# A fused four-layer graph network: the GAT keys' logit parts by token, turned into rows by transposes, in another order of the round

## The reference, cut to what matters

```python
def _L3_gnn_ref(h, adj_matrix, W, a):
    Wh = jnp.einsum('bnf,fo->bno', h, W)
    a1, a2 = (a[:Fout, 0], a[Fout:, 0])
    s1 = Wh @ a1                       # the query's part of a logit
    s2 = Wh @ a2                       # the key's part
    e = s1[:, :, None] + s2[:, None, :]
    e = jnp.where(e >= 0, e, ALPHA * e)
    e = jnp.where(adj_matrix[None] == 0, -jnp.inf, e)
    attention = jax.nn.softmax(e, axis=-1)
    h_prime = jnp.einsum('bij,bjo->bio', attention, Wh)
    return h_prime
```

## Time and profile before

| | before |
|---|---|
| median of 3 runs | 2158.94 us |
| the profiled execution: its time, and its span from first to last instruction | 2162.29 us, 2160.5 us |
| PE busy | 2017.1 us, 93% |
| DVE busy | 1749.8 us, 81% |
| ACT busy | 1451.9 us, 67% |
| mean granted TensorE clock | 0.98 |

### The profile page before, as it was taken

One profiled execution on the slowest core, in us unless ns is written; L12 is line 12 of the kernel. 1 busy time (PEld: TensorE's weight loads), 2 busy tenths in 40 slices (PEclk: granted clock), 3 DMA queues, 4 the chain that ended last, 5 costly groups with the idle time before them and its releaser, 6 DMA issues. The chain is left out here.

```text
span 2160.5 us, 86772 instructions
## 1 busy us (share of the span) xinstructions
PE 2017.1 (93%) x37609; PEld 1780.4 (82%) x37609; DVE 1749.8 (81%) x4987; ACT 1451.9 (67%) x4411; POOL 187.0 (9%) x259
## 2 busy tenths in 40 slices
PE   6979769999999999999999999999999999999986
PEld 3434358989898989889898989898989998899985
DVE  6779767888888888888888888888888888888865
ACT  5657336767776777667676776676767766676775
POOL 2000000000001000100010000101010001000000
PEclk9989789999999999999999999999999999999998
DMA  7847300000100001000100010000000010000000
GB/s 277 289 173 267 107 11 12 13 12 3 41 3 22 3 3 42 12 12 3 42 13 12 3 41 13 12 3 28 16 22 3 3 42 12 12 3 12 3 12 12
DMA packets 36825, 87.85 MB, mean 41 GB/s; under 512 B 2416, under 2 KB 26992, under 8 KB 32752
## 3 DMA queue, kind: packets, MB, share of 16 engines
q1 hardware_dynamic: 36464, 82.56, 11.0%
HBM read 52.15 MB, written 30.41 MB: 38 GB/s over the span
## 5 line engine op out<-in xcount | busy, mean ns | idle before, releaser
L1443 ACT ACTIVATE pool_mem<-ps,lstm_b 128x64 f32<-128x64 f32 (+2 forms) x2496 | 603.9, 354 | 191.8 <-PE ps L252 186.4
L250 PE MATMUL ps<-hl_a,w_hi 128*128 128x64 f16 (+2 forms) x3776 | 545.6, 215 | 31.9 <-DVE hl_a L623 16.0
L251 PE MATMUL ps<-hl_a,w_hi 128*128 128x64 f16 (+2 forms) x3776 | 544.3, 215 | 0.0
L252 PE MATMUL ps<-hl_a,w_lo 128*128 128x64 f16 (+2 forms) x3776 | 543.8, 215 | 0.0
L250 PEld LDWEIGHTS ps<-hl_a,w_hi 128*128 128x128 f16 x3776 | 350.5, 98 | 64.0 <-DVE hl_a L623 17.1
L251 PEld LDWEIGHTS ps<-hl_a,w_hi 128*128 128x128 f16 x3776 | 350.2, 98 | 24.4 <-issue 3.0
L252 PEld LDWEIGHTS ps<-hl_a,w_lo 128*128 128x128 f16 x3776 | 350.2, 98 | 24.4 <-issue 3.0
L250 PE MATMUL ps<-hl_b,w_hi 128*128 128x84 f16 (+2 forms) x2112 | 366.3, 228 | 2.5 <-ACT pool_mem L1443 1.7
L251 PE MATMUL ps<-hl_b,w_hi 128*128 128x84 f16 (+2 forms) x2112 | 366.0, 228 | 0.0
L252 PE MATMUL ps<-hl_b,w_lo 128*128 128x84 f16 (+2 forms) x2112 | 364.3, 228 | 0.0
L250 PE MATMUL ps<-pool_mem,w_hi 128*128 128x64 f16 (+2 forms) x3072 | 352.4, 200 | 2.2 <-DVE pool_mem L1716 2.0
(11 more groups left out here) (244 smaller groups left out, 4402.1 us busy)
## 6 DMA issues: line engine op xcount, KB each, us to landing
xa<-in_x SPq DMA_DIRECT2D x32, 512.0 KB, 5.5
h_scratch<-pool_mem SPq DMA_DIRECT2D x14, 1024.0 KB, 4.3
pool_mem<-h_scratch SPq DMA_DIRECT2D x14, 1024.0 KB, 6.8
pool_mem<-in_wpack SPq DMA_DIRECT2D x16, 704.0 KB, 4.3
out<-xb SPq DMA_DIRECT2D x16, 512.0 KB, 3.4
o_scratch<-act_in SPq DMA_DIRECT2D x14, 512.0 KB, 3.2
act_in<-o_scratch SPq DMA_DIRECT2D x14, 512.0 KB, 5.4
row<-in_rows SPq DMA_DIRECT2D x1, 1408.0 KB, 11.4
```

The source lines that it names most:

```text
L250: nc.tensor.matmul(o, l[0], r[0], start=first, stop=False, skip_group_check=True)
L251: nc.tensor.matmul(o, l[0], r[1], start=False, stop=False, skip_group_check=True)
L252: return nc.tensor.matmul(o, l[1], r[0], start=False, stop=last, skip_group_check=True)
L1443: op = nc.scalar.activation(gates[s][h][:, g, m * w:(m + 1) * w], gate_place(s, h, g, m, w), ACT.Tanh, bias=lstm_b[:, bias:bias + 1], scal ...
```

## The change

The keys' parts are no longer made as rows. `wa` holds the two columns side by side, and the 12 small matmuls of `gat` have two moving columns, so that s1 and s2 of a token lie next to each other on the token's partition. DVE scales all four numbers of a half (two blocks of 128 tokens by two parts) in one instruction. A new step `gat_keys` has PE turn s2 into rows: a transpose of the one column, broadcast to 128, into the same PSUM bank. ACT adds s1 as before, without a scale. ACT takes Wh out in step `gat`, ahead of the logits, which now belong to `gat_keys`; so do the leaky ReLU and the mask on DVE. The setup makes `wa` in place of `wa1` and `wa2`.

```diff
-                    for k in range(KT):
-                        product(ps[s][:, BANK_B[h], 0:HTOK], (wa2[:, 0, k, :], wa2[:, 1, k, :]),
-                                (src[:, 0, k, tokens(h)], src[:, 1, k, tokens(h)]), k == 0, k == KT - 1)
                     for b in range(HALF):
                         a = h * HTOK + b * P
                         for k in range(KT):
-                            mm = product(ps[s][:, BANK_B[h], HTOK + b:HTOK + b + 1],
+                            mm = product(ps[s][:, BANK_B[h], HTOK + 2 * b:HTOK + 2 * b + 2],
                                          (src[:, 0, k, a:a + P], src[:, 1, k, a:a + P]),
-                                         (wa1[:, 0, k:k + 1], wa1[:, 1, k:k + 1]), k == 0, k == KT - 1)
+                                         (wa[:, 0, k, :], wa[:, 1, k, :]), k == 0, k == KT - 1)
                     mm.then_inc(gat_ps.of(s, h), 1)
                     dense(s, h, src, h * HTOK, "w3", BANK_A[h]).then_inc(gat_ps.of(s, h), 1)
+
+                def gat_keys(s, n, h):
+                    pe.wait_ge(*logit_ok.at(s, n, h, "parts"))
+                    for b in range(HALF):
+                        mm = nc.tensor.transpose(ps[s][:, BANK_B[h], b * P:(b + 1) * P],
+                                                 part_of(s, h, b, 1).broadcast_to([P, P]), ident[:, :])
+                    mm.then_inc(gat_ps.of(s, h), 1)
...
                 def gat_logits(s, n, h):
 
-                    act.wait_ge(*logit_ok.at(s, n, h, "s1"))
+                    act.wait_ge(*gat_ps.at(s, n, h, "keys"))
                     for b in range(HALF):
                         op = nc.scalar.activation(logit[s][h][:, b, :], ps[s][:, BANK_B[h], b * P:(b + 1) * P], ACT.Identity,
-                                                  bias=s1[s][h][:, b:b + 1], scale=-UNSCALE)
+                                                  bias=part_of(s, h, b, 0))
...
                     elif base == "gat":
+                        take_wh(s, n, h)
+                    elif base == "gat_keys":
                         gat_logits(s, n, h)
-                        take_wh(s, n, h)
...
+                def gat_parts(s, n, h):
+                    at = 8 + (s * HALVES + h) * HALF * 2
+                    dve.wait_ge(*gat_ps.at(s, n, h, "parts"))
+                    nc.vector.tensor_scalar(small[:, at:at + 2 * HALF], ps[s][:, BANK_B[h], HTOK:HTOK + 2 * HALF], -UNSCALE, None,
+                                            ALU.mult).then_inc(logit_ok.of(s, h), 1)
...
-0:turn_state.0 1:mix1.0 1:inp1.1 1:cell1.1 0:gat.1 0:norm_l2.0 1:hid1.1 0:gat_exps.1 1:gcn1.0 0:turn_att.1 0:turn_xc.0
...
+1:mix0.0 1:inp0.1 0:turn_xc.1 0:turn_state.0 1:cell0.1 1:gcn0.0 0:gat.1 0:gat_keys.1 1:mix1.0 1:hid0.1 0:gat_exps.1
+1:inp1.1 1:cell1.1 0:norm_l2.0 1:hid1.1 0:turn_att.1 1:gcn1.0 0:turn_xc.0 0:gat_mix.1 0+norm_y 1:inp0.0 1:cell0.0
```

More of the change, by code:

```diff
@@ L89 @@
[L89 to L103, removed]
+1:cheb.1 0:pack3.1 0:cell3.0 1:conv.1 0:hid3.0 1:v.0 1:q.0 1:k.0 1:norm_g1.1 0:inp4.1 0:pack3.0 1:xa_bias.1
@@ new lines @@
+1:turn_x1.1 0:cell4.1 1:scores.0 0:inp4.0 0:cell4.0 0:hid4.1 1:v.1 1:q.1 1:k.1 0:hid4.0 0:inp5.0 1:scores.1 1:exps.0
+1:exps.1 0:inp5.1 0:cell5.1 0:cell5.0 0:hid5.1 1:turn_probs.1 0:inp6.1 1:attend.1 0:hid5.0 0:cell6.1 0:hid6.1
+1:attn_out.1 1:norm_g2.1 1:turn_probs.0 0:inp6.0 0:pack4.1 1:attend.0 0:cell6.0 1:turn_x2.1 0:inp7.1 0:cell7.1
+0:hid6.0 1:attn_out.0 0:hid7.1 0:inp8.1 0:pack4.0 1:norm_g2.0 1:mlp_up.1 1:gelu_split.1 0:cell8.1 0:inp7.0 0:hid8.1
+1:turn_x2.0 0:cell7.0 1:mlp_down.1 0:hid7.0 0:inp9.1 0:cell9.1 1:norm_g3.1 1:norm_l1.1 1:mlp_up.0 1:gelu_split.0
@@ new lines @@
+0:hid9.1 0:inp10.1 0:inp8.0 0:cell8.0 1:mix0.1 0:hid8.0 1:mlp_down.0 0:cell10.1 1:norm_g3.0 0:hid10.1 1:gcn0.1
+0:inp9.0 1:mix1.1 1:norm_l1.0 0:cell9.0 0:hid9.0 0:turn_state.1 1:gcn1.1 0:inp10.0 0:cell10.0 0:hid10.0 0:norm_l2.1
+1:mix0.0 1:inp0.1 0:turn_xc.1 0:turn_state.0 1:cell0.1 1:gcn0.0 0:gat.1 0:gat_keys.1 1:mix1.0 1:hid0.1 0:gat_exps.1
+1:inp1.1 1:cell1.1 0:norm_l2.0 1:hid1.1 0:turn_att.1 1:gcn1.0 0:turn_xc.0 0:gat_mix.1 0+norm_y 1:inp0.0 1:cell0.0
+0:norm_l3.1 0:gat.0 0+turn_y.1 0:gat_keys.0 1:inp2.1 1:cell2.1 1:hid0.0 0:gat_exps.0 1:inp1.0 1:hid2.1 0:turn_att.0
@@ new lines @@
+0+norm_l0.1 1:cell1.0 0:gat_mix.0 1:hid1.0 0+cheb.1 1:inp3.1 0:norm_l3.0 0+turn_y.0 0+conv.1 0+norm_l0.0 0+norm_g1.1
+1:inp2.0 1:cell2.0 1:cell3.1 0+cheb.0 1:hid2.0 1:inp3.0 0+xa_bias.1 0+turn_x1.1 0+conv.0 0+norm_g1.0 1:cell3.0
+0+xa_bias.0 0+v.1 0+q.1 0+turn_x1.0 1:hid3.0 0+k.1 1:pack3.0 0+v.0 1:hid3.1 0+scores.1 1:inp4.0 1:cell4.0 0+exps.1
+0+q.0 1:pack3.1 0+k.0 1:hid4.0 1:inp5.0 0+turn_probs.1 0+scores.0 0+attend.1 1:inp4.1 0+exps.0 1:cell5.0 0+attn_out.1
+0+turn_probs.0 1:hid5.0 1:cell4.1 0+norm_g2.1 1:inp6.0 0+attend.0 1:cell6.0 1:hid6.0 0+turn_x2.1 1:hid4.1 1:inp5.1
@@ new lines @@
+0+attn_out.0 0+norm_g2.0 1:pack4.0 0+mlp_up.1 0+gelu_split.1 1:cell5.1 0+turn_x2.0 1:inp7.0 1:cell7.0 1:hid7.0
+0+mlp_down.1 1:hid5.1 1:inp6.1 0+norm_g3.1 0+mlp_up.0 1:inp8.0 0+norm_l1.1 0+gelu_split.0 1:cell8.0 1:cell6.1 1:hid8.0
+1:hid6.1 0+mix0.1 1:pack4.1 0+mlp_down.0 1:inp9.0 1:cell9.0 1:inp7.1 1:cell7.1 1:hid7.1 1:hid9.0 1:inp10.0 1+norm_y
+0+norm_g3.0 1:inp8.1 1:cell8.1 1:cell10.0 0+norm_l1.0 1:hid10.0 1:hid8.1 1:inp9.1 0+gcn0.1 1:turn_state.0 0+mix0.0
+0+mix1.1 1:norm_l2.0 1:cell9.1 1:hid9.1 0+gcn0.0 1:turn_xc.0 1:inp10.1 1:cell10.1 1:gat.0 1:hid10.1 1:gat_keys.0
@@ L104 @@
+0+mix1.0 1:turn_state.1 1:gat_exps.0 0+gcn1.1 1:turn_att.0 1:norm_l2.1 0+gcn1.0 1:gat_mix.0 1:turn_xc.1 0+inp0.1
+0+cell0.1 1:norm_l3.0 1+turn_y.0 0+inp0.0 0+cell0.0 0+hid0.1 1+norm_l0.0 0+inp1.1 0+cell1.1 0+hid1.1 1:gat.1 1+cheb.0
+0+hid0.0 0+inp1.0 1:gat_keys.1 0+cell1.0 1+conv.0 0+inp2.1 1:gat_exps.1 0+hid1.0 1:turn_att.1 0+cell2.1 1:gat_mix.1
+0+hid2.1 0+inp3.1 1:norm_l3.1 1+norm_g1.0 0+inp2.0 0+cell2.0 1+turn_y.1 0+hid2.0 1+norm_l0.1 0+cell3.1 0+hid3.1
+1+xa_bias.0 1+turn_x1.0 0+inp3.0
 """.split()
@@ L192, in build @@
         lstm_b = sb("lstm_b", [P, SKIPS * GATES // P])
-        wa1 = sb("wa1", [P, 2, KT], F16)
-        wa2 = sb("wa2", [P, 2, KT, P], F16)
+        wa = sb("wa", [P, 2, KT, 2], F16)
         bn1 = sb("bn1", [P, 2, HT])
@@ L917, in build @@
             up_ps = Signal("up_ps", "m01 m23")
-            gat_ps = Signal("gat_ps", "logits wh att")
+            gat_ps = Signal("gat_ps", "parts wh keys att")
             feat_hi = Signal("feat_hi", " ".join(FEATS))
@@ L1039, in build, with part_of @@
             pack_hl = {3: hl_b, 4: hl_a}
-            s1 = [[small[:, 8 + BLK * s + HALF * h:8 + BLK * s + HALF * (h + 1)] for h in range(HALVES)]
-                  for s in range(STREAMS)]
+            def part_of(s, h, b, of_key):
+                at = 8 + ((s * HALVES + h) * HALF + b) * 2 + of_key
+                return small[:, at:at + 1]
             xc = x1
@@ L1347, in _ @@
                          "mix1": mix_h, "gcn1": gcn_second, "turn_state": turn_state, "turn_xc": turn_xc,
-                         "gat": gat_dense, "turn_att": turn_att, "gat_mix": gat_mix}
+                         "gat": gat_dense, "gat_keys": gat_keys, "turn_att": turn_att, "gat_mix": gat_mix}
                 def run(name, s, n):
@@ L1798, in run @@
                     elif base == "gat":
+                        gat_parts(s, n, h)
+                    elif base == "gat_keys":
                         gat_logits(s, n, h)
```

14 lines of the change are left out of this document (4 added, 10 removed).

## The result

| | before | after |
|---|---|---|
| median of the runs beside each other (4 each) | 2159.25 us | 2141.55 us (2140.46 to 2143.51) |
| ratio, 95% interval | | 0.9919 [0.9901, 0.9936] |
| profiled execution, its span | 2162.29, 2160.5 us | 2141.88, 2140.1 us |
| opening, its start up to the first round | 104.5 us, PE busy 76.1 | 110.8 us, PE busy 78.7 |
| one round (mean of seven) | 231.3 us | 227.2 us |

The change is faster by 17.7 us, 8 more than the forecast of 9.7. In the profiled executions the difference is 20.4: the seven rounds lost 28.3, the opening gained 6.3 and the closing 1.7 (the last 0.1 is the setup). Of all the executions reported here one, of the old rows in the new list, took 3380.69 us at a granted clock of 0.56; no ratio counts it.

A forecast was written before the change was run, and what follows sets the result against it. PE was taken as the bound, busy 224.6 of 232 us a round. Terms -12.5 + 11.2 - 5.6 - 9.9 + 5.6 + 1.5 = -9.7 us gave 2149.2 us for the runs; range 2139 to 2164.

The forecast's parts named there:

- PE's work, −12.5: In gat and turn_att: row matmuls gone (0.66 us), two transposes added (0.27), net 0.39 us a half, 32 halves: -12.5 us.
- The wait at `turn_att`, +11.2: PE waits for the exponentials 3.25 us a round, 1.6 more than now, over seven rounds: +11.2 us, bounds +8 and +18.
- beside it PE has: PE work set beside ACT's queue before turn_att: 2.92 us against 4.36, and 2.97 against 4.23, leaving waits 1.4 and 1.3.
- `gat_mix`, −5.6, and conv.1, inp2.0, turn_y.0 of stream 0, −9.9: PE waits that go: 0.8 us a round at gat_mix, 1.4 at the other three, as more PE work stands before them.
- Tight places, +5.6: New waits where the new list leaves less between steps (inp0.0, v.0, turn_x1): 0.8 us a round, +5.6, bounds 0 and +15.
- The clock, 0 in the sum: Granted clock falls behind turn_att.1 of stream 0, about 4.8 us for three rounds; no gain from this in the forecast's sum.
- The ends, +1.5: In the closing, stream 1's last two gat start their logits later, +1.5 us for both; the setup counted 0.
- ACT's chain becomes the bound: Rival: all four halves wait before turn_att, 5.6 us a round; +6.4, 2165.3 us; chance 0.18.
- The transposes cost what their row says: Rival: 0.273 us each, saving 0.11 a half, 3.5 us in place of 12.5; 2158.2; shares chance 0.14 with another rival.
- Nothing shows: Rival: waits refill each gain, PE idles 7.4 + 1.5 us a round; 2158.9 us; shares chance 0.14 with another rival.
- The clock rival: Rival: gains come whole, no tight place waits, turn_att waits 2.8, clock stays up (-4.8); -23.3, 2135.6 us; chance 0.15.

The follow-up runs named there:

- the old rows in the new list: Kernel before, keys' parts still rows by six matmuls, under the changed kernel's step order, Wh in gat, logits in gat_keys: 2157.62 us, 0.9989 of the kernel before.
- The early Exp in the kernel before: Kernel before, plus a one-column Exp on ACT in turn_state so that the table load happens there: 2148.07 us, 0.9948 of the kernel before.
- two other runs: The old rows in the new list, 2157.62 us; and the changed kernel with ACT taking Wh behind the logits, 2148.99 us.
- the run with the old ends: Changed kernel, rounds untouched, opening and closing steps in the order of the list before: 2133.3 us, 0.9866 of the kernel before.

## Why the prediction was right, and where not

The direction, and the mechanism of most terms, held; the time lay inside the range, but below the forecast's own 2144 to 2155, which had the largest chance. That it lay inside the range is in part luck: two errors of opposite sign. Against the span the forecast was −9.7 and −20.4 came: rounds 18.6 better, ends 8.0 worse.

- **PE's work, −12.5: right.** 0.30 us for twelve matmuls, with one column or two. A pair of transposes takes 0.22 from its start to the next matmul's in two halves, and 0.36 in the two where mix1 follows, 0.29 in the mean where 0.27 was counted: 0.37 a half net. Of the 2.5 by which PE's busy time fell a round, 1.5 is this, 0.7 the clock, and 0.3 has no shown cause. Doubling the transposes confirms the size.
- **The wait at `turn_att`, +11.2: wrong in size, the largest error.** The chain was right: 4.36 and 4.23 worked out, 4.27 and 4.24 measured. The waits were 1.10, 0.59, 0.12 and 0: 1.8 a round where 3.25 was taken and 2.8 worked out. The step that failed is "beside it PE has". In the second place PE was held on its way by a wait of its own (0.41 at turn_state.1), and such a wait is time that the chain gets free. In the first place there was none; there, and in the second too, PE had more than was counted: the transposes take 0.36 and not 0.27, and the last matmul is busy for 0.16 more than the distance from start to start (2.18 for inp1, where 2.02 was counted), while a wait begins only at its end. I added waits as if each were by itself, and then added 0.45 for lateness of ACT or DVE. The one more trip over PE, which the term was argued from, is not what the wait measures: with the old rows in the new list, which have no such trip, the first wait was 1.45. Measured, the term is +1.1 over seven rounds.
- **`gat_mix`, −5.6, and conv.1, inp2.0, turn_y.0 of stream 0, −9.9: right.** Two of four waits went, and those three are gone from every round.
- **Tight places, +5.6: near in sum, wrong in place.** inp0.0 waits 0.25 and v.0 0.37; turn_x1 0.05. But turn_y.0 of stream 1 (0.67), cheb.1 of stream 0 (0.41) and turn_state.1 (0.41) are new and not in the working, and of the waits of about 2.4 a round that it did not count (cheb.0 0.72 and 0.22, conv.1, turn_x1.1 and others) most went. In sum these other waits rose from 2.4 to 3.0 a round, 3.8 us in seven, and that they came near 5.6 is luck.
- **The clock, 0 in the sum: wrong.** The rival had 4.8 us for it, and that part came true: three falls before, none after. PE's busy time was 224.9 in the three rounds with a fall and 223.3 in the other four, so 1.6 each and 4.8 in all. The early Exp in the kernel before shows the wait ahead of the earlier trace rows as the cause. It belonged in the likeliest case: the sum already had this wait at 1.4 against 1.66, and I gave its clock no price. With 1.45 in two other runs there was no fall either.
- **The ends, +1.5: wrong.** +8.0, of which 6.5 is the order of the list at the ends, as the run with the old ends shows, and not Wh or the logits. I had looked at one chain of the closing and nothing of the opening.
- **The rivals.** "ACT's chain becomes the bound" wanted over 5.2 us of `turn_att` waits a round: 1.8. "The transposes cost what their row says": out. "Nothing shows": out for this kernel, yet close to what the list alone did. The clock rival had 8.0 for the waits and nothing for the ends; its −23.3 was nearer to the −20.4 than the forecast, by its clock, and by errors that cancel, so partly by luck.

Summed up with measured terms: rounds −10.4 (the work, 28 halves), +1.1 (`turn_att`), −12.0 (other waits), −4.8 (clock), −2.2 (rest, cause not shown), −28.3 in all; ends +8.0, setup −0.1.

**Still open:** why the clock falls in only some rounds with the same wait, and in only some openings with the same steps; and what the rest of 0.3 us of PE's busy time a round is.
